# Turning every second unit of scaled q by a transposing DMA instead of on TensorE

## The reference

```python
x = x + attn(layernorm(x));  x = x + ffn(layernorm(x))
# attn
q = relu(x @ Wq); k = relu(x @ Wk); v = x @ Wv          # (32 heads, 2048, 64)
kv = einsum('bhsd,bhse->bhde', k, v)
out = einsum('bhsd,bhde->bhse', q, kv) / clip(einsum('bhsd,bhd->bhs', q, k.sum(s)), 1e-6)
return out @ Wo + bo
# ffn
scores = x @ gate_w.T + gate_b + bias; top 2, softmax
y = silu(x @ w1[e].T + b1[e]) @ w2[e].T + b2[e], summed over the two experts with their gates
```

## Time and profile before

| | |
|---|---|
| median of three runs | 993.48 us (991.97 to 993.57) |
| profiled execution | 993.69 us, of which the span is 992.0 us |
| mean granted TensorE clock | 0.999 |
| PE | 979.3 us busy, 99% |
| PE weight load | 823.5 us, 83% |
| DVE | 714.3 us, 72% |
| ACT | 553.7 us, 56% |
| POOL | 248.5 us, 25% |

### The profile page before, as it was taken

The page is one execution under the profiler, slowest core; times in us unless marked ns, Lnnn a source line. Parts: engine busy times, 40 slices in busy tenths (PEclk is TensorE's granted clock), DMA queues, the critical chain, the costliest instruction groups (busy, mean ns, idle before and its releaser), DMA issues.

```text
span 992.0 us, 17230 instructions
## 1 busy us (share of the span) xinstructions
PE 979.3 (99%) x4863; PEld 823.5 (83%) x4863; DVE 714.3 (72%) x1594; ACT 553.7 (56%) x1376; POOL 248.5 (25%) x407
## 2 busy tenths in 40 slices
PE   9999999999999999999999999999999999999997
PEld 7888888888888888888788888888888888888896
DVE  7888665665656676757878787888887786677674
ACT  5445544444445445865556556655555796565553
POOL 1000000000000002221644343444443573433334
PEclk9999999999999999999999999999999999999999
DMA  7012654555555531333221111111114765787773
GB/s 267 4 40 86 212 170 170 170 184 187 188 188 190 188 122 64 107 123 96 86 72 57 53 53 53 53 53 60 56 43 138 230 195 95 119 115 110 119 114 49
DMA packets 121048, 116.15 MB, mean 117 GB/s; under 512 B 47049, under 2 KB 95354, under 8 KB 120866
## 3 DMA queue, kind: packets, MB, share of 16 engines
q1 hardware_dynamic: 111746, 98.51, 32.7%
q0 software_dynamic: 9248, 16.95, 9.1%
HBM read 42.91 MB, written 64.14 MB: 108 GB/s over the span
## 4 chain that ended last, share of the span: by engine, by line
PE 89%; DVE 4%; ACT 3%; DMA 2%; issue 1%; POOL 0%; POOLq 0%; ACTq 0%; DVEq 0%; SPq 0%
PE pK L1739 13%; PE pK L1741 13%; PE pK L1740 13%; PE pA L1739 8%; PE pA L1741 8%; PE pA L1740 8%; PE pX L1739 5%; PE pX L1741 5%; PE pX L1740 5%; PE pA L1873 3%; DMA out<-y,slot_token 2%; PE pT L1819 2%; ACT w_hi L1152 1%; PE pX L2108 1%; PE pT L1754 1%
## 5 line engine op out<-in xcount | busy, mean ns | idle before, releaser
L1006 ACT ACTIVATE qs<-q,nrec 128x64 f32<-128x64 f32 x512 | 129.6, 335 | 88.3 <-DVE nrec L1437 88.2
L622 POOL TENSOR_TENSOR wv_lo<-wv_in,wv_hi 128x512 fp32r<-128x512 f32 x4 | 5.2, 1298 | 403.2 <-ACT wo_hi L927 403.2
L1739 PE MATMUL pA<-k_hi,xn_hi 128*128 128x512 f32 x256 | 101.0, 394 | 0.5 <-DVE k_lo L1312 0.5
L1739 PE MATMUL pK<-wq_hi,xnT_hi 128*128 128x512 f32 x256 | 100.4, 392 | 0.0
L1739 PE MATMUL pK<-wk_hi,xnT_hi 128*128 128x512 f32 (+1 forms) x256 | 100.0, 391 | 0.1
L1741 PE MATMUL pK<-wq_hi,xnT_lo 128*128 128x512 f32 x256 | 99.9, 390 | 0.0
L1741 PE MATMUL pA<-k_hi,xn_lo 128*128 128x512 f32 x256 | 99.8, 390 | 0.0
L1740 PE MATMUL pK<-wk_lo,xnT_hi 128*128 128x512 f32 (+1 forms) x256 | 99.8, 390 | 0.0
L1740 PE MATMUL pK<-wq_lo,xnT_hi 128*128 128x512 f32 x256 | 99.7, 389 | 0.0
L1740 PE MATMUL pA<-k_lo,xn_hi 128*128 128x512 f32 x256 | 99.7, 389 | 0.0
L1741 PE MATMUL pK<-wk_hi,xnT_lo 128*128 128x512 f32 (+1 forms) x256 | 99.6, 389 | 0.0
(11 more groups left out here) (302 smaller groups left out, 2457.3 us busy)
## 6 DMA issues: line engine op xcount, KB each, us to landing
xr_dram<-zero SPq DMA_DIRECT2D x10, 3584.0 KB, 12.8
w_in<-in_ffn_w SPq DMA_DIRECT2D x22, 256.0 KB, 4.0
w_in<-in_ffn_w SPq DMA_DIRECT2D x8, 704.0 KB, 6.5
xn<-in_attn_hidden_states SPq DMA_DIRECT2D x16, 256.0 KB, 5.6
wv_in<-in_attn_Wv SPq DMA_DIRECT2D x16, 256.0 KB, 2.8
wo_in<-in_attn_Wo SPq DMA_DIRECT2D x16, 256.0 KB, 3.0
wk_in<-in_attn_Wq SPq DMA_DIRECT2D x4, 1024.0 KB, 5.7
xnT_dram<-xnT SPq DMA_DIRECT2D x4, 1024.0 KB, 11.7
```

Of the source, the lines that this page charges most:

```text
L1006: i = nc.scalar.activation(qs[:, s], q[:, s], ACT.Copy, scale=nrec[:, b * HC + h:b * HC + h + 1])
L1739: nc.tensor.matmul(dst, lhs[0], rhs[0], start=start, stop=False)
```

## The change

Units 17, 19, ..., 61 no longer go through `transpose_qs`. ACT splits the scaled unit into two 16-bit planes (`put_qs_planes`), SP turns both planes by one transposing DMA from SBUF to SBUF (`turn_qs`), DVE joins them to 32-bit words in one copy (`join_planes`), and high and low parts are taken from there (`act_joined`, `dve_joined`). The products of odd units run one unit later than before, so that PE's order in a pair with even unit m is project_q(m), times_m(m - 3), project_q(m + 1), times_m(m - 2), transpose_qs(m). The bank of pA that odd units used holds the sums of every second tile (`o_bank`). Two of the eight gate scores move from the end of one tile to the next. Buffers of the planes lie where `w1_in` 2 and 3 were loaded, so these loads come at the end. Tiles 4 and 5 stand outside the loops, and SP's loop is written out.

```diff
+    qs_planes = sb("qs_planes", 2 * CW, 156 * KB, U16)
+    qsT_words = sb("qsT_words", CW, 156 * KB)
+    qsT_planes = sb("qsT_planes", 2 * CW, 158 * KB, U16)
...
+        turned = lambda p, t: 2 * t - 8 + p
+        o_bank = lambda odd: pX[:, :] if odd else pA[:, 1536:2048]
...
+            def turn_qs(nth):
+                sp.wait_ge(qs_planes_ready, nth)
+                if nth > 1:
+                    sp.wait_ge(qsT_joined, nth - 1)
+                sp.dma_start_transpose(qsT_planes[:, :].rearrange("p (c n) -> p c n", n=P), qs_planes[:, :]).then_inc(s_qsT, 16)
+
             def tile_io(t):
-                if not (isinstance(t, int) and t == 1):
+                if t > 4:
+                    turn_qs(turned(0, t))
+                if t > 1:
                     next_xnT(t)
+                if t > 3:
+                    turn_qs(turned(1, t))
                 sp.wait_ge(x2_ready, t)
...
-            load_w1(0, 4, s_w1a)
+            load_w1(0, 2, s_w1a)
...
+            turn_qs(turned(1, NT - 1))
+            sp.wait_ge(q_put, NC * NT - 1)
+            load_w1(14, 15, s_w1b)
             sp.wait_ge(x2_ready, NT - 1)
             sp.dma_start(out[(NT - 2) * P:(NT - 1) * P, :], x2[:, :]).then_inc(x2_stored, 16)
-            sp.wait_ge(q_put, NC * NT - 1)
-            load_w1(14, 15, s_w1b)
+            sp.wait_ge(qsT_lo_ready, NC * NT - 2)
+            load_w1(2, 4, s_w1q)
...
+            def put_qs_planes(m):
+                act.wait_ge(qs_ready, m + 1)
+                act.wait_ge(qsT_lo_ready, m - 1)
+                nc.scalar.copy(planes(qs_planes), words(qs[:, CW:2 * CW])).then_inc(qs_planes_ready, 1)
+
+            def act_joined(m, nth):
+                act.wait_ge(qsT_joined, nth)
+                act.wait_ge(o_put, m - 1)
+                nc.scalar.copy(qsT_hi[:, CW:2 * CW], qsT_words[:, :]).then_inc(qsT_hi_ready, 1)
...
             def act_tile(t, b):
+                for p in range(2):
+                    m = 4 * t + 2 * p
+                    act_q(m, 0)
+                    if not (first and p == 0):
+                        act_qsT(m - 2, 0, 2 * t + (8 + p))
+                    if p == 0 and not final:
                         act_qx(t + 1, 1 - b)
+                    if p == 1:
+                        put_planes(t - 2)
+                    act_qs(m, 0)
+                    if p == 1:
                         sqrt_var(NT + t - 1)
...
+                        act_q(m + 1, 1)
+                        act_joined(m - 1, turned(p, t))
+                    act_qs(m + 1, 1)
+                    if not (final and p == 1):
+                        put_qs_planes(m + 1)
...
+            def join_planes(nth):
+                dve.wait_ge(s_qsT, 16 * nth)
+                nc.vector.tensor_copy(words(qsT_words[:, :]), planes(qsT_planes)).then_inc(qsT_joined, 1)
+
+            def dve_joined(m):
+                dve.wait_ge(qsT_hi_ready, m + 1)
+                lo(qsT_lo[:, CW:2 * CW], qsT_words[:, :], qsT_hi[:, CW:2 * CW]).then_inc(qsT_lo_ready, 1)
...
             def dve_tile(t, b):
+                for p in range(2):
+                    m = 4 * t + 2 * p
...
+                        dve_q(m, 2 * p, 0, put=2 * t + (8 + p))
+                        dve_qsT(m - 2, 0)
+                    if p == 0:
+                        if not final:
                             dve_qx(t + 1, 1 - b)
+                        if not first:
+                            join_planes(turned(0, t))
+                        dots(t - 2, 4 if first else 2, 6)
+                    else:
+                        x2_stats(t - 1, 1 - b)
+                        join_planes(turned(1, t))
...
+                        dve_q(m + 1, 2 * p + 1, 1, copied=2 * t - 8 + p)
+                        dve_joined(m - 1)
+                    if p == 0:
+                        dots(t - 2, 6, E)
                         put_scores(t - 2)
+                    else:
+                        put_slot8(t - 2, b)
                         layernorm2(t - 1)
+                        dots(t - 1, 0, 2)
...
             def pe_tile(t, b):
-                for c in range(NC):
-                    m = 4 * t + c
-                    project_q(m, t, c, b)
-                    transpose_qs(m - 1, (c - 1) % 2)
-                    if c == 2:
-                        pe.wait_ge(x2_ready, t)
-                    if c == 3:
+                for p in range(2):
+                    m = 4 * t + 2 * p
+                    project_q(m, t, 2 * p, b)
+                    if isinstance(t, int) and t == 4 and p == 0:
+                        transpose_qs(15, 1)
+                    else:
+                        times_m(m - 3, (2 * p - 3) % 4, 1, o_bank(1 - b))
+                    project_q(m + 1, t, 2 * p + 1, b)
+                    if p == 1:
                         rank(t - 2, b)
-                    times_m(m - 2, (c - 2) % 4, c % 2, pX[:, :])
+                        pe.wait_ge(x2_ready, t - 1)
+                    times_m(m - 2, (2 * p - 2) % 4, 0, o_bank(b if p else 1 - b))
+                    transpose_qs(m, 0)
...
+            times_m(4 * NT - 3, 1, 1, pX[:, :])
+            pe.wait_ge(x2_ready, NT - 1)
+            transpose_qs(4 * NT - 1, 1)
             w_transpose(0)
             w_transpose(1)
-            transpose_qs(4 * NT - 1, 1)
             times_m(4 * NT - 2, 2, 0, pX[:, :])
             times_m(4 * NT - 1, 3, 1, pX[:, :])
```

More of the change, by code:

```diff
@@ L533, in _ @@
             sp.wait_ge(wq_lo_ready, 2 * NC)
-            load_w1(0, 4, s_w1a)
+            load_w1(0, 2, s_w1a)
             sp.wait_ge(gw_put, 1)
             load_w1(4, 6, s_w1a)
-            with sp.Fori(3, NT - 2) as t:
+            for t in range(3, NT - 1):
                 tile_io(t)
-            tile_io(NT - 2)
+            turn_qs(turned(0, NT - 1))
             def load_w2(e):
@@ L1424, in _, with dve_q @@
             heads = lambda a: a.rearrange("p (h d) -> p h d", h=HC)
-            def dve_q(m, c, b):
-                if not (isinstance(m, int) and m < 2):
+            def dve_q(m, c, b, put=None, copied=None):
+                if put is not None:
+                    dve.wait_ge(qsT_put, put)
+                elif copied is not None:
+                    dve.wait_ge(qs_planes_ready, copied)
+                elif m > 1:
                     dve.wait_ge(qsT_put, m - 1)
@@ L1447, in dve_qx, with residual @@
                 lo(xnT_lo[:, s], xnT_in[:, :], xnT_hi[:, s]).then_inc(xnT_lo_ready, 1)
-            def residual(t):
+            def residual(t, odd=None):
                 dve.wait_ge(o_put, 7 if isinstance(t, int) and t == 0 else 4 * t + 4)
@@ L1453, in residual @@
                     dve.wait_ge(x2_stored, 16 * t)
-                o = pA[:, 512:1024] if isinstance(t, int) and t == 1 else pX[:, :]
+                o = o_bank(odd) if odd is not None else pA[:, 512:1024] if t == 1 else pX[:, :]
                 nc.vector.tensor_tensor(x2[:, :], o, xb[:, :], ALU.add).then_inc(x2_ready, 1)
@@ L1543, in put_slot8, with x2_stats @@
                 nc.vector.tensor_tensor(slot8[b][:, :], pT[:, 0:E], ebase[:, :], ALU.add).then_inc(slot_ready, 1)
-            def x2_stats(t):
-                residual(t)
+            def x2_stats(t, odd=None):
+                residual(t, odd)
                 dve.wait_ge(x2_ready, t + 1)
@@ L1585, in dve_tile @@
             def dve_tile(t, b):
[L1586 to L1593, removed]
[L1594 to L1596 removed]
+                first, final = (isinstance(t, int) and t == n for n in (4, NT - 1))
+                for p in range(2):
+                    m = 4 * t + 2 * p
+                    if first and p == 0:
+                        dve_q(m, 0, 0)
+                    else:
[3 more added lines that the diff above has]
+                        if not final:
+                            dve_qx(t + 1, 1 - b)
+                        if not first:
[4 more added lines that the diff above has]
+                        join_planes(turned(1, t))
+                    if first and p == 0:
+                        dve_q(m + 1, 1, 1)
+                        dve_qsT(15, 1)
+                    else:
+                        dve_q(m + 1, 2 * p + 1, 1, copied=2 * t - 8 + p)
+                        dve_joined(m - 1)
+                    if p == 0:
+                        dots(t - 2, 6, E)
                         put_scores(t - 2)
[L1598 removed]
+                    else:
+                        put_slot8(t - 2, b)
                         layernorm2(t - 1)
[L1600 to L1604 removed]
+                        dots(t - 1, 0, 2)
+            dve_tile(4, 0)
+            dve_tile(5, 1)
+            with dve.Fori(3, NT // 2 - 1) as h:
                 for b in range(2):
@@ L1608, in _ @@
             dve_tile(NT - 1, 1)
+            dve_qsT(4 * NT - 2, 0)
             dve_qsT(4 * NT - 1, 1)
-            dots(NT - 2, 4, E)
+            dots(NT - 2, 2, E)
             put_scores(NT - 2)
@@ L1992, in _ @@
                 times_m(10 + c, (c - 2) % 4, c % 2, pX[:, :])
```

(4 more changed lines are left out.)

33 lines of the change are left out of this document (18 added, 15 removed).

## The result

| | before | after |
|---|---|---|
| median | 993.28 us (991.97 to 993.57, 4 runs) | 981.04 us (980.45 to 981.55, 4 runs) |
| profiled execution | 993.69 us, span 992.0 | 981.01 us, span 979.3 |

The ratio is 0.9879, with a 95% interval of 0.9862 to 0.9896: 1.2% faster, a gain of 12.2 us by the medians. The forecast was 983.2 us with a range from 981.3 to 992.0.

A forecast was written before the change was run, and what follows sets the result against it. PE (TensorE) was taken as the bound: profiled 993.69 - 10.1 (transposes) - 0.5 (stall) = 983.1 us, or 982.9 from the median of 993.48; with 0.3 added for small waits, 983.2 us. Range 981.3 to 992.0.

The forecast's parts named there:

- PE bounds the stretch: Between 460 and 770 us PE leads and other engines follow; removing PE instructions shortens it until another engine's slack is used.
- A group costs 0.44 us, 23 of them 10.1: On PE, the four transposes of each removed odd unit cost 0.44 us by pitch; 23 groups save 10.1 us.
- The check: PE's tile summed as 4 x (2.72 + 2.77 + 0.44) plus 0.14 for rank matmuls: 23.86 us against 23.79 read.
- The stall of the last odd unit, 0.5: The last odd unit's transposes wait 0.49 us for ACT; the new order removes this, counted as -0.5 us.
- 0.3 us for unseen small waits: Allowance of 0.3 us added to the sum for small waits in a chain with 0.5 to 1 us of slack.
- The turn lands after 3.3 us and is hidden: SP's transposing DMA of the planes, bounds 3.1 and 5.6 us, taken as 3.3; nothing then stops PE.
- The join takes 0.70, and the collision moves to it: DVE's join of planes 0.70 us; GpSimd's addition may slow it instead of q's product, priced at nothing, 1.1 worst.
- DVE has 1.0 us of idle left in a tile: DVE's 3.4 us idle per tile, less a tile 0.9 shorter and 1.5 more work, leaves 1.0 us: tight, not the bound.
- The circle: Loop through both joins, dots, q, scaling, planes and turns: 13.95 + 2X against a 22.9 us tile, holding to X = 4.5.
- X: Time for SP's turn to land, from the end of ACT's plane copy; taken as 3.3 us.
- my layout: Timetable of a tile's pairs from projection m's start T, PE untroubled: first join 6.6, second about 19.3, next turn due T+25.5.
- Rival 1: The turn replaces the transposes as bound: beyond X = 4.5 each us costs 22; 1007 us at 5.6; chance 0.14.

The follow-up runs named there:

- e1: Kernel after with four identity transposes put back on PE at each of the 23 spots, between projection m+1 and product m-2; 992.19 us, ratio 0.9987.
- e9: Kernel after with a 64 KB store and its wait (1.53 us) ahead of only the 11 turns issued in a tile's second pair; 998.15 us, ratio 1.0054.
- e6: Kernel after with each DVE join done twice, the second behind a wait for the first; 991.68 us, ratio 0.9977.
- e8: Kernel after with each DVE join done three times; 1009.67 us, ratio 1.0157.
- e10: Kernel after with a 64 KB store and its wait (1.53 us) ahead of only the 12 turns issued in a first pair; 981.59 us, ratio 0.9887.

## Where the prediction held and where it failed, point by point

- *PE bounds the stretch.* Right. PE never waits in the tiles that the change edits, and its pitch decides.
- *A group costs 0.44 us, 23 of them 10.1.* This is the step that failed. The price by pitch and not by duration was right in kind, but it was read from the first two pitches behind one group and multiplied by 23. The rest of the block was left out: in the earlier trace rows the product behind the group takes 2.85 us where a block without one takes 2.72, so the group costs 0.36 + 0.13 = 0.49. The check had this in it, as 2.77 for a product, and took the 0.05 over 2.72 for the product's own. Measured, the change gave 0.96 us a tile, 0.48 a group, 11.1 us for the 23: 1.0 more than the term. (e1's 0.45 is a little lower because one of its two groups stands beside the rank matmuls, where the stream is interrupted anyway.)
- *The stall of the last odd unit, 0.5.* Right; no such row after.
- *0.3 us for unseen small waits.* Not needed: no new wait of PE is in the tiles. In the sum this allowance pointed the wrong way.
- *The turn lands after 3.3 us and is hidden.* Right: 3.1, hidden in all tiles. Choosing the cleaner of the two rows kept the forecast near; the other row's 5.6 was no more excluded by the trace, so there was luck in it. With one of the two turns at 5.54 (e9) the change already loses.
- *The Trainium skill's figure.* (VectorE: DVE Perf Modes, The three transpose paths: 1309 ns for one 128x128 block by DMA.) Eight blocks land here in 3.0 to 3.1 us together, so the trace doesn't bear out a price per block in series. The same page (Rules for kernel authors) says to use TensorE for a 128x128 transpose if a destination in PSUM will do. In this kernel, where TensorE is the full engine and the transfer is off its path, the DMA was faster by 1.2%.
- *The join takes 0.70, and the collision moves to it.* 0.75, and 1.11 where it meets GpSimd. The loss moved from 1.09 on the q product to 0.36 on the join, since the join starts 0.8 us into the addition. I had priced it at nothing, with 1.1 as the worst; the sum needed nothing for it.
- *DVE has 1.0 us of idle left in a tile.* It has 1.56, but only 0.73 can be used (e6, e8). "Not the bound" was right, the reasoning wrong: I took idle time for slack.
- *The circle is 13.95 + 2X, holds up to 4.5, and every us beyond costs 22.* Wrong as a mechanism, though it did no harm to the time, since X was 3.1. I followed one chain through both turns. The chain that binds first passes through one turn only; in the other half it goes through ACT's copy of the next q, which waits behind the plane copy, and through DVE's own work. I had written that this delay was "the part that counts", and my layout had DVE at the second join at 19.3, 12.7 us after the first at 6.6 (measured 12.57); the circle left this leg out. With it, and 6.2 from there to the next turn at 25.5, the layout would have given 22.9 - 12.7 - 6.2 = 4.0 as the limit. The measured limit for the turn from the second pair is 4.1 to 4.3; beyond it a us costs 11 us, and 22 only when both turns bind, from about 5.1 on. Rival 1's price at X = 5.6 for both turns was still about right: 13.7 + 11.2 = 24.9 us a tile, 22 us in all by the rule fitted above (an estimate, no run has it), where I had 24.
- *The size.* On the profiled executions the forecast with its allowance is 993.69 - 10.1 - 0.5 + 0.3 = 983.4, and 981.01 was measured. The 2.4 us are 1.0 for the groups, 0.3 for the allowance, 0.2 of other small gains, and 0.9 for the third part of the kernel, which the change doesn't touch and which differs by as much from kernel to kernel. The low end, 981.3, was only 1.9 below the forecast. It allowed for hardly more than this scatter, and for no error in a term taken from one group's rows and multiplied by 23. Without either the 1.0 or the 0.9 the time would have been inside; that the miss is only 0.26 us says little about the mechanism.

## What to carry to other kernels

Price an instruction on a full TensorE by the pitch it takes in the stream, from the block in front of it to the end of the block behind it, and check it by putting it back: the durations overstated this saving by more than twice, and the first two pitches understated it by a tenth. Before calling another engine's idle time slack, follow the round that its idle rows belong to. An engine that idles for a neighbour whose own queue got longer has less room than its idle sum says, and a latency that looks hidden twice in a loop may have one tight place and one loose one. A difference of a microsecond in a part of the program that the change doesn't touch belongs in the range.

## What the runs showed of the hardware

- A transposing DMA of 128x1024 16-bit values from SBUF to SBUF held SP for 1.24 us and landed 3.0 to 3.1 us after issue in 21 of the 23 turns of the kernel after, also with GpSimd's scatters of rows beside it (issued at 603.24 and 604.63, turn at 602.63). The first took 3.8 us and the last 4.4, with a load of weights issued 1.3 us behind it. In e9 the load of transposed x came 2.1 us behind it, and it took 4.0. The cause of the longer times isn't tested; but a delayed transfer may meet other traffic than the one on time, so its lateness can be more than the delay.
- A transpose of a 128x128 32-bit block lasts 0.27 us. In TensorE's stream at a granted clock of 1.00 each took 0.11 to 0.12 us, in fours or twos, and an interruption of the stream by a group 0.04 more, since the matmuls of the block behind started up to 0.236 us apart and not 0.227.
- A 128x1024 16-bit copy within SBUF on DVE took 0.75 us alone and 1.11 beside GpSimd's 1.29 us addition, of which 0.49 lay beside it; the 32-bit product with two inputs from SBUF, in the earlier trace rows, lost 1.09 with 1.23 beside it. In all such meetings from 500 us on in the kernels before and after and in e10, where the addition had started first, with 0.34 to 1.23 us side by side, DVE lost the time side by side less 0.13 to 0.15 us, and the addition kept its 1.28 to 1.30.
